# Graph-relation layer on one Trainium2 core: rank-one matmuls against sums carried through DRAM, with part of each batch computed one batch later

## The reference

```python
h = relu(layernorm(x))                       # x: 16 batches of 512 nodes x 128 features
HW[r] = h @ W[r, :F] + c[r]                  # c[r] = W_edges[r] @ W[r, F:], one row of 128 per relation
A = [adj, adj, shift, adj.T, adj.T, shift.T, eye]         # relations 0..6, adj: 16 x 512 x 512, fp32
out = x + max over r of (A[r] @ HW[r]) + b
```

## Time and profile before

| what | value |
|---|---|
| runs, median (lowest to highest) | 246.71 us (246.6 to 247.39) |
| profiled execution: span from the first to the last instruction | 245.5 us |
| busy: PE, DVE, ACT, POOL | 98%, 72%, 66%, 64% of the span |
| steady batches, on PE | 14.46 us each |
| DMA | 26.07 MB, mean 106 GB/s, mean busy share 33.8% of 16 engines |

### The profile page before, as it was taken

How to read it: one execution, slowest core, us unless ns; L and a number is a source line. 1 busy time by engine, 2 the same in 40 slices (tenths; PEclk the granted TensorE clock), 3 DMA queues, 4 the chain that set the end, 5 groups by cost and what they waited for, 6 DMA issues and landing times.

```text
span 245.5 us, 4869 instructions
## 1 busy us (share of the span) xinstructions
PE 240.3 (98%) x1199; PEld 183.5 (75%) x1199; DVE 176.1 (72%) x395; ACT 162.8 (66%) x452; POOL 156.4 (64%) x232
## 2 busy tenths in 40 slices
PE   7999999999999999999999999999999999999995
PEld 5686877868778686877868687786877778687772
DVE  4779879686766867677696766769576686856544
ACT  3878985857669386765938667594867859476130
POOL 3358899676693966759396685938668494866000
PEclk9999999999999999999999999999999999999998
DMA  6916073415161440516134061622506152010011
GB/s 194 333 28 218 17 240 123 136 46 172 46 212 46 131 125 24 190 43 209 47 107 150 5 208 43 183 74 87 169 0 214 43 154 102 0 35 7 0 45 43
DMA packets 27826, 26.07 MB, mean 106 GB/s; under 512 B 1720, under 2 KB 19624, under 8 KB 27816
## 3 DMA queue, kind: packets, MB, share of 16 engines
q1 hardware_dynamic: 27815, 25.95, 33.8%
HBM read 21.75 MB, written 4.19 MB: 106 GB/s over the span
## 4 chain that ended last, share of the span: by engine, by line
PE 93%; DVE 3%; DMA 2%; SPq 0%; issue 0%
PE rel_ps L738 13%; PE at_ps L707 11%; PE rel_ps L740 10%; PE rel_ps L739 10%; PE bwd_ps L738 6%; PE bwd_ps L740 6%; PE bwd_ps L739 6%; PE fwd_ps L738 6%; PE fwd_ps L739 6%; PE fwd_ps L740 6%; PE rel_ps L797 6%; PE misc_ps L715 3%; PE misc_ps L733 3%; DMA a_sb<-in_adj 2%; PE rel_ps L892 1%; DVE at_lo L506 0%
## 5 line engine op out<-in xcount | busy, mean ns | idle before, releaser
L258 POOL TENSOR_TENSOR a_lo<-a_sb,a_hi 128x512 fp32r<-128x512 f32 x60 | 76.4, 1293 | 25.1 <-ACT a_hi L360 25.1
L506 DVE TENSOR_TENSOR at_lo<-at_ps,at_hi 128x512 fp32r<-128x512 f32 x61 | 41.9, 688 | 29.4 <-ACT at_hi L368 29.3
L368 ACT ACTIVATE at_hi<-at_ps 128x512 fp32r<-128x512 f32 x61 | 36.4, 597 | 26.9 <-PE at_ps L707 25.2
L535 DVE TENSOR_TENSOR best<-rel_ps,best 128x512 f32<-128x512 f32 x63 | 43.0, 683 | 3.5 <-PE rel_ps L797 0.2
L360 ACT ACTIVATE a_hi<-a_sb 128x512 fp32r<-128x512 f32 x64 | 39.8, 624 | 3.8 <-DMA a_sb<-in_adj 3.8
L532 DVE SCALAR_TENSOR_TENSOR best<-rel_ps,c_col,best 128x512 f32<-128x512 f32 x32 | 23.9, 746 | 20.0 <-PE rel_ps L740 16.5
L265 POOL TENSOR_TENSOR h_lo<-h_sb,h_hi 128x512 fp32r<-128x512 f32 x15 | 19.4, 1297 | 28.4 <-DVE h_hi L500 28.4
L707 PEld LDWEIGHTS at_ps<-ident,a_sb 128*128 128x128 f32 x240 | 29.7, 141 | 8.3 <-issue 0.7
L707 PE MATMUL at_ps<-ident,a_sb 128*128 128x128 f32 x240 | 35.8, 272 | 0.0
L386 ACT ACTIVATE ht_hi<-misc_ps 128x512 fp32r<-128x512 f32 x16 | 9.6, 600 | 34.2 <-PE misc_ps L715 34.2
L738 PE MATMUL bwd_ps<-a_hi,h_hi 128*128 128x512 f32 x64 | 28.1, 439 | 0.0
(11 more groups left out here) (108 smaller groups left out, 485.5 us busy)
## 6 DMA issues: line engine op xcount, KB each, us to landing
a_sb<-in_adj SPq DMA_DIRECT2D x64, 256.0 KB, 4.2
x_sb<-in_x SPq DMA_DIRECT2D x16, 256.0 KB, 2.8
out<-o_sb SPq DMA_DIRECT2D x15, 256.0 KB, 2.2
w_sb<-in_L_gnn_W SPq DMA_DIRECT2D x1, 448.0 KB, 6.4
bias_sb<-in_L_gnn_b SPq DMA_DIRECT2D x1, 256.0 KB, 6.7
out<-o_sb SPq DMA_DIRECT2D x2, 128.0 KB, 1.8
we_sb<-in_L_gnn_W SPq DMA_DIRECT2D x1, 56.0 KB
wedge<-in_L_gnn_W_edges SPq DMA_DIRECT2D x1, 0.4 KB, 4.6
```

Source lines behind the costliest of these rows:

```text
L258: pool.tensor_tensor(a_lo[q][:, j, :], a_sb[q][:, j, :], a_hi[q][:, j, :].bitcast(fp32), ALU.subtract).then_inc(a_lo_ready[j], 1)
L368: act.activation(at_hi[q][:, i, :], at_bank(b, i)[:], ACT.Copy, accum_out=sums[q][:, 1, i:i + 1]).then_inc(at_hi_ready[i], 1)
L506: dve.tensor_tensor(at_lo[q][:, i, :], at_bank(b, i)[:], at_hi[q][:, i, :].bitcast(fp32), ALU.subtract).then_inc(at_lo_ready[i], 1)
L535: dve.tensor_tensor(best[:], rel_ps[BANK[r]][:], best[:], ALU.max).then_inc(joined[r], 1)
```

## The change

- The four rank-one matmuls of a batch, `split_sums`, `rows_of_sums`, `c_rows`, `ident_r` and all tiles for them go.
- In their place the [128, 8] tile of sums is turned by one fp32 transpose (128 columns, output on 8 partitions), copied to SBUF by ACT (`take_sums`, 8x128), stored to a DRAM tensor of 4 KB, and read back by a DMA that broadcasts these 1024 values to all 128 partitions (`sum_all`, 512 KB). SP waits for the store's landing before it issues the read.
- ACT then writes sums times c into the relation's PSUM bank (`fill`, 128x512 from SBUF, scale a [128,1] pointer), and the three passes of the relation accumulate onto it (start=False).
- The four relations along edges of a batch run one step later, under the next batch's matmuls. `best` becomes a pair. ORDER is EYE, FWD, BWD.
- PE's order in a step alternates the phases. Orders on ACT, DVE and POOL are rewritten to match; batches 0 and 1 have orders of their own.
- SP: a step is store(b-2), reload x, reload adj, spread_sums. At the start SP waits for the first chunk of adj before it issues any further load, and loads W ahead of the second batch's adj.

```diff
+            def spread_sums(k, q):
+                b = 2 * k + q
+                sp.wait_ge(sum_rows_ready, b + 1)
+                sp.dma_start(sums_dram[q][:, :], sum_rows[q][:]).then_inc(sums_stored[q], 16)
+                sp.wait_ge(sums_stored[q], 16 * (k + 1))
+                sp.dma_start(sum_all[q][:].rearrange("p t n -> p (t n)"),
+                             sums_dram[q].rearrange("s p -> (s p)").unsqueeze(0).to_broadcast([P, 2 * N])
+                             ).then_inc(sums_spread[q], 16)
...
+            sp.wait_ge(a_loaded[0][0], 16)
             load_x(0, 1)
+            sp.dma_start(w_sb[:], W[:, 0:F, :].rearrange("r f o -> f r o")).then_inc(w_loaded, 16)
+            for j in range(C):
+                load_a(0, 1, j)
...
+            def step(k, q, more, stored=True):       # SP
+                if stored:
+                    store(k - 1, q)
+                if more:
+                    reload_x(k, q)
+                    reload_a(k, q)
+                spread_sums(k, q)
...
             def step(k, q, left):                    # POOL, batches from 2
+                    if left:
+                        reciprocal_std(*after(k, q))
+                    add_bias(k, q)
+                    split_a(k, q, 2)
+                    split_a(k, q, 3)
                 if left:
                     ahead = after(k, q)
+                    split_h(*ahead)
                     split_a(*ahead, 0)
                     split_a(*ahead, 1)
...
+            def fill(k, q, r, to, after_it, cols=slice(0, N)):      # ACT
+                act.wait_ge(sums_spread[q], 16 * (k + 1))
+                act.activation(to[:, cols], sum_all[q][:, 0 if r in FWD else 1, cols], ACT.Copy,
+                               scale=c_col[:, r:r + 1]).then_inc(after_it, 1)
...
             def step(k, q, left):                    # ACT, batches from 2, put together
                 round_at(k, q, 2); round_at(k, q, 3)
+                if not left: take_sums(k, q, at_ps[0])
                 join_first(k, q)
+                act.wait_ge(joined[BWD[0]], b - 1);  fill(*prev, FWD[0], ...)
+                act.wait_ge(joined[EYE[0]], b + 1);  fill(*prev, FWD[1], ...)
                 if left: normalise(*ahead)
+                act.wait_ge(joined[FWD[0]], b);      fill(*prev, BWD[0], ...)
+                if left: round_at(*ahead, 0); take_sums(k, q)
+                act.wait_ge(joined[FWD[1]], b);      fill(*prev, BWD[1], ...)
                 if left: round_at(*ahead, 1); round_ht(*ahead)
                 round_fwd(k, q)
                 if left: round_a(*ahead, 0..3); round_bwd(k, q)
...
             def step(k, q, left):                    # DVE, batches from 2, put together
                 finish(k - 1, q); split_at(k, q, 2); split_at(k, q, 3); split_bwd(*prev)
                 join(k, q, EYE[1]); join(*prev, FWD[0]); round_h(*ahead)
                 join(*prev, FWD[1]); split_at(*ahead, 0); moments(k + 1, q)
                 join(*prev, BWD[0]); split_at(*ahead, 1); mean_and_variance(q)
                 join(*prev, BWD[1]); split_ht(*ahead); join(k, q, EYE[2]); split_fwd(k, q)
...
             def step(k, q, left):                    # PE
+                fwd(k, q, 0)
+                eye(k, q, EYE[0])
+                fwd(k, q, 1)
+                if not left:
+                    pe.wait_ge(at_lo_ready[2], B)
+                    turn_sums(k, q, at_ps[0])
+                eye(k, q, EYE[1])
+                fwd(k, q, 2)
+                along(*prev, FWD[0])
+                fwd(k, q, 3)
+                along(*prev, FWD[1])
+                if left:
+                    turn_a(*ahead, 0)
+                    turn_a(*ahead, 1)
+                    turn_h(*ahead)
+                    pe.wait_ge(joined[EYE[1]], b + 1)
+                    turn_sums(k, q)
                 bwd(k, q, 0)
+                along(*prev, BWD[0])
                 bwd(k, q, 1)
+                along(*prev, BWD[1])
                 bwd(k, q, 2)
+                eye(k, q, EYE[2])
                 bwd(k, q, 3)
                 if left:
                     turn_a(*ahead, 2)
                     turn_a(*ahead, 3)
+                    turn_best(*prev, b + 2)
```

More of the change, by code:

```diff
@@ L99, in gnn_layer @@
         sums = pair(sb, "sums", [P, 2, C])
-        sum_parts = pair(sb, "sum_parts", [P, G, QUARTER], fp32r)
+        sum_rows = pair(sb, "sum_rows", [S, P])
+        sum_all = pair(sb, "sum_all", [P, 2, N])
         fwd_hi = sb("fwd_hi", [P, N], fp32r)
@@ L272, in add_bias @@
                 pool.tensor_tensor(xb_sb[q][:], x_sb[q][:], bias_sb[:], ALU.add).then_inc(xb_ready, 1)
[L274 to L296, removed]
             def first_step():
                 ahead = (0, 1)
-                pool.wait_ge(parts_zeroed, 1)
-                split_sums(0, 0)
+                split_a(0, 0, 2)
+                split_a(0, 0, 3)
+                reciprocal_std(*ahead)
                 pool.wait_ge(w_hi_ready, 1)
@@ L418, in first_step @@
                 act.activation(w_hi[:], w_sb[:], ACT.Copy).then_inc(w_hi_ready, 1)
-                round_bwd(0)
+                take_sums(0, 0)
+                round_at(*ahead, 0)
+                round_at(*ahead, 1)
+                normalise(*ahead)
+                act.wait_ge(c_ready, 1)
+                join_first(0, 0)
+                round_fwd(0, 0)
+                round_ht(*ahead)
+                round_at(*ahead, 2)
+                round_at(*ahead, 3)
                 round_a(*ahead, 0)
@@ L460, in _ @@
-            act.wait_ge(ident_ready, 1)
-            act.activation(ident_r[:], ident[:], ACT.Copy).then_inc(ident_r_ready, 1)
+                    round_ht(*ahead)
+                    round_fwd(k, q)
+                    for j in range(C):
+                        round_a(*ahead, j)
+                    round_bwd(k, q)
+                else:
+                    round_fwd(k, q)
+            act.wait_ge(consts_ready, 1)
+            act.activation(neg_mean[1][:], minus_one[:], ACT.Copy)
             def normalise_chunk(j):
@@ L712, in turn_h @@
                 pe.wait_ge(h_ready, b + 1)
[L713 to L721 removed]
+                if isinstance(b, int) and b == 1:
                     pe.wait_ge(ht_lo_ready, 1)
@@ L723, in turn_sums @@
                 else:
-                    pe.wait_ge(out_ready, b)
-                pe.matmul(misc_ps[:, 0:P], sum_parts[q][:].rearrange("p g k -> p (g k)"), ident_r[:],
-                          start=True, stop=True).then_inc(sums_turned, 1)
-            def turn_best(k, q):
+                    wait(pe, out_ready, b - 2)
+                    wait(pe, ht_lo_ready, b)
+                for j in range(C):
+                    last = pe.transpose(turn_ps[:, j * P:(j + 1) * P], h_sb[q][:, j, :], ident[:])
@@ new lines, in eye, with along @@
+                passes(rel_bank(b, r)[:], w_hi[:, r, :], w_lo[:, r, :], ht_hi[q][:], ht_lo[q][:],
+                       True, True).then_inc(rel_done[r], 1)
+            def along(k, q, r, to=None):
+                b = 2 * k + q
+                to = rel_ps[BANK[r]] if to is None else to
+                pe.wait_ge(filled[r], b + 1)
+                if r in FWD:
+                    hi, lo = fwd_hi, fwd_lo
+                    pe.wait_ge(fwd_hi_ready, b + 1)
+                    pe.wait_ge(fwd_lo_ready, b + 1)
+                else:
+                    hi, lo = bwd_hi, bwd_lo
@@ L810, in first_step @@
             def first_step():
                 ahead = (0, 1)
-                for j in range(C):
-                    bwd(0, 0, j)
+                bwd(0, 0, 0)
+                bwd(0, 0, 1)
                 turn_h(0, 0)
+                bwd(0, 0, 2)
+                fwd(0, 0, 0)
+                bwd(0, 0, 3)
+                turn_sums(0, 0)
+                turn_a(*ahead, 0)
+                fwd(0, 0, 1)
+                fwd(0, 0, 2)
+                turn_a(*ahead, 1)
+                fwd(0, 0, 3)
```

529 lines of the change are left out of this document (228 added, 301 removed).

## The result

| | us | n |
|---|---|---|
| before, median | 246.62 | 5 |
| changed, median (lowest to highest) | 233.91 (233.12 to 235.21) | 5 |
| ratio, 95% interval | 0.9485 (0.9456 to 0.9514) | |
| predicted | 232.1, range 228 to 240 | |

The change saves 12.7 us. The profiled execution of the changed kernel took 235.21 us, with a span of 233.3. It is the longest of the five; the spans of the others are 231.2 to 232.0. So 1.3 us or more of what the profile shows above the prediction belongs to this execution and not to the median.

A forecast was written before the change was run, and what follows sets the result against it. PE's queue was taken as the bound. Start 37.9, steps 2 to 14 173.8 and last step with tail 19.2 gave a span of 230.9; with 1.2 around it, 232.1 us, range 228 to 240.

The forecast's parts named there:

- steps 2 to 14: Steady part: 13 steps of 13.37 us of PE work each, 173.8 us, without stalls.
- last step and end: Last matmul ends 15.4 us after the step begins; with joins and tail, 19.2 us.
- around the span: Time of a run outside the profiled span, taken as 1.2 us from the median of 246.71.
- PE's queue is the bound: Steady batches: PE's own work sets 14.46 us a batch; dropping the rank-ones removes 1.25 us a batch.
- The turn of the sums: PE's transpose of the sums onto 8 partitions: 0.11 to 0.27 us, 0.27 taken.
- The order in the steady part: Steady-step walk: nothing stops PE; fills ready 0.5 us or more ahead, fwd_lo thinnest at 0.35 us.
- Rival 1: ACT and DVE handoffs replace the rank-ones, stopping PE 0.5 us every step: 239 us; chance 0.17.
- The transfer: Sums' store and broadcast through DRAM: issued 7.7, landing about 13.6 on the step's clock, with 2.6 us of room.
- Rivals 2 and 3: Steady broadcast late: one transfer slow, 238 to 246 us, chance 0.08; both late, 280 us, chance 0.05.
- The start: Everything before batch 2: PE work plus stalls, batch 2 beginning at 37.9 us; bounds 33.5 and 40.7.
- Stalls by the same walk: PE waits before batch 2: 1.5 us in batch 0, 2.9 in batch 1, where the first broadcast lands late.
- The end: Last step: fwd_lo late by 0.9 us because DVE joins the last eye first.

The follow-up runs named there:

- padded broadcasts: Changed kernel with the broadcast writing the sums two (1 MB) or three times (1.5 MB) per partition, fills reading the last copy: 236.61 and 249.76 us.
- both edits: Changed kernel with batch 1's bias addition moved early on POOL and the first batch's sums store and broadcast ahead of reloads on SP: 229.51 us.
- without the route: Changed kernel without the sums' store, broadcast and four fills, PE waiting for free banks instead: 236.05 us.
- bias_early: Changed kernel with batch 1's bias addition moved from behind its four a_lo to the end of POOL's first step: 232.25 us.
- 1 MB broadcast: Changed kernel with the broadcast writing the sums twice into each partition and fills reading the second copy: 236.61 us.
- sums first alone: Changed kernel with only SP's first store and broadcast of sums put ahead of x and adj of batch 2: 236.06 us.

## Why the prediction was right, point by point

The time came out in the range, 1.8 us above the forecast, by the mechanism given: PE's queue is shorter by the rank-ones and nothing takes their place in the steady part. That the number is as near as this is partly luck, since two misses of nearly the same size, in the steady batches and at the start, cancel. Against the profiled execution the terms are:

| term | forecast | measured | difference |
|---|---|---|---|
| batch 2 begins | 37.9 | 40.85 | +2.95 |
| steps 2 to 14 | 173.8 | 213.26 - 40.85 = 172.4 | -1.4 |
| of it: 13 batches | 13.37 each | 13.15 each | -2.85 |
| of it: first passes at the low clock | 0 | 1.5 | +1.5 |
| last step and end | 19.2 | 233.3 - 213.26 = 20.0 | +0.8 |
| span | 230.9 | 233.3 | +2.4 |
| around the span | 1.2 | 235.21 - 233.3 = 1.9 | +0.7 |

The last row is no cost of the change. Most runs of the kernel before also take 1.8 us beyond their span (246.99 with 245.2, 247.4 with 245.6); the 1.2 came of setting the median beside the span of an execution that was longer than the median one. In the median execution of the change, 233.91 with a span of 232.0, the miss of 1.8 is 1.1 of span and 0.7 of this.

**PE's queue is the bound.** Right. Without the rank-ones 18.2 us go, 1.26 a batch against 1.25 reckoned.

**The turn of the sums.** Wrong. I took 0.27, by the gap around the 32-row matmuls, and it costs 0.11, the low end. Fewer output columns don't cost what fewer rows cost. This is 0.16 of the 0.22 us by which the batch is shorter than forecast. The Trainium skill (TensorEngine Tiling (Array Packing), Tiling Modes) lets a change of tiling mode drain TensorE. By the 32-row pairs the trace agrees (0.16 us). Around the 8-column transpose it shows no such gap, so either that one is no change of mode or its drain costs nothing here. The other 0.06 us of the 0.22 is not explained; the old order without rank-ones takes 13.20.

**The order in the steady part.** Right, handoff by handoff. No PE row there has a bracket. ACT's fills stand 0.5 us or more ahead of PE. fwd_lo, the thinnest, is ready at 120.89 and wanted at 121.26 (0.37, forecast 0.35). Rival 1 did not happen.

**The transfer.** Right. The store and the broadcast land 5.8 us after the store's issue, forecast 5.9, and the broadcast within 0.5 us of its median. Only at the start is the store slower, behind x and adj in flight: 3.7 us from its issue at 19.34 to the broadcast's at 23.07, and 4.6 from 35.30 to 39.89. The Trainium skill (HBM Reference, Latency) names 2 us for an access under high load; in the steady batches, at 163 GB/s, nothing here shows such a spread. Rivals 2 and 3 did not happen, but the padded broadcasts show how near: 3.5 us more brings them, 1.7 doesn't.

**The start.** Wrong, and the largest miss. The step that failed is the second half of "Stalls by the same walk: 1.5 in batch 0, 2.9 in batch 1". Batch 1 begins at 22.11, where the sum gives 21.6 (it starts from 9.5, though its row has 9.66; the changed kernel's first adj matmul is at 9.17), and then takes 40.85 - 22.11 = 18.7 us, that is 5.6 of stalls and not 2.9. The walk followed the first broadcast to its place (ACT's fill, 26.70 in the trace, 26.3 forecast) and stopped there. It never took x of batch 3 through SP: that load waits for POOL's bias, which the change left behind four lo parts, and it came at 32.91. Moving one POOL instruction and one SP step gives 4.4 us back, more than the 1.8 by which the forecast was missed.

**The clock.** Not in the sum at all. Behind the idle time ahead of batch 2 come 1.5 us of slower passes. That is the profiled execution; by their mean clocks two of the other four (0.998 and 1.000) have little or nothing of it.

**The end.** Nearly right: fwd_lo late by 0.85 us as reckoned (0.9). The last join starts 0.4 us later than forecast, behind others on DVE.

Why the change gets less than the 18.2 us: in spans of the profiled executions, 233.3 - 226.6 = 6.7 us (the medians differ by 5.2, since the change's other executions are shorter). Batch 2 begins 40.85 - 38.59 = 2.3 later; the low clock is 1.5; 13 steady batches give back 0.65; and from the start of the last batch to the end it is 20.0 against 226.6 - 210.12 = 16.5, so 3.5 more. That sums to 6.65. Of the 3.5, four relations of batch 14 that now run in the last step are 4 x 0.70 = 2.8. The deferral owes this at the end and should earn it at the start, where batches 0 and 1 do four relations less before batch 2. With the order of the change that credit was waited away; with both edits batch 2 begins 2.1 us before that of the kernel without rank-ones, and the time, 229.5, is within 0.8 us of it.

## What to carry to other kernels

When work is taken from a full engine, check the steady part by its slots, and then give the first batches a walk of their own over every load of every queue, each with what frees its buffer: a load held up by one POOL instruction, and a small store queued behind big loads, cost here 4.4 us, a third of what the change won. A small operand in another shape can cost more than a full one, so look at the gaps around it and not at its duration. Work put off by one step is paid at the end and is a gain only if the start uses the room.

## What the runs showed of the hardware that was not expected

- A matmul over 128 rows is cheaper between 128-row matmuls than one over 32 rows: the pair 0.46 against 0.625 us, 5.0 us in all. An fp32 transpose of 128 columns onto 8 partitions costs 0.11 us between full ones, like one onto 128.
- One 4 KB row read 128 times from DRAM lands in 3.6 us, 2 copies in 5.3, 3 in 7.1: 1.75 us for each 512 KB, 300 GB/s, the rate at which x and adj came in the earlier trace rows.
- Short waits were at times followed by the 1.2 GHz level. After 0.89 and 0.69 us of idle (changed kernel) PE ran its passes at 0.43 us until 44.6, after 2.39, 0.89 and 0.23 (without the route) until 45.6; with one wait of 0.38 us at that place (bias_early) not at all. The length of the waits alone doesn't decide it: with the 1 MB broadcast the granted clock was 1.00 behind a wait of 2.69 us (at 29.62) and behind 0.58 and 0.69 us at the place of the change's (40.64 and 41.96), but 0.50 from 8 to 10 behind one of 1.25 us for adj (at 7.05).
- Waits taken away ahead of a fixed obstacle gathered in front of it: 2.39 us in one piece without the route, 2.73 with the sums first alone. Both kernels came out 2.1 us slower than the change, by causes that the runs show only in part.
